# Transformer layer on one core: weight maxima taken across partitions by PE turns and a DRAM round trip instead of POOL, filler matmuls in the front, and a hint on the loop's branch

## The reference

```python
x = x + layernorm(attention(layernorm(x)))
x = x + layernorm(ffn(layernorm(x)))

def attention(x):                       # 16 heads of 32; latent sizes 128
    c_kv, c_q = x @ W_dkv + b_dkv, x @ W_dq + b_dq
    v = c_kv @ W_uv + b_uv
    q = rotary(c_q @ W_qr + b_qr)       # the non-rotary part has width 0
    k = rotary(x @ W_kr + b_kr)
    return softmax(q @ k.T / sqrt(32)) @ v @ W_o + b_o

def ffn(x):                             # 512 -> 2048 -> 512, fwht = Walsh-Hadamard
    x = fwht(x * SU_ug) / 64
    up, gate = x @ W_up.T * (Wscale_ug[:2048] * 64), x @ W_gate.T * (Wscale_ug[2048:] * 64)
    return (fwht(silu(gate) * up * SU_dp) / 64) @ W_down.T * (Wscale_dp * 64)
```

## Time and profile before

| | us |
|---|---|
| median of three runs | 2049.63 |
| the execution that was profiled | 2057.66 |
| its span, first to last instruction | 2055.8 |
| first loop iteration starts on PE | 404.2 |
| last loop iteration ends on PE | 1738.9 |

### The profile page before, as it was taken

One profiled execution on the slowest core, in us unless ns is written; L12 is line 12 of the kernel. 1 busy time (PEld: TensorE's weight loads), 2 busy tenths in 40 slices (PEclk: granted clock), 3 DMA queues, 4 the chain that ended last, 5 costly groups with the idle time before them and its releaser, 6 DMA issues.

```text
span 2055.8 us, 59485 instructions
## 1 busy us (share of the span) xinstructions
PE 1884.7 (92%) x24328; PEld 1368.8 (67%) x24328; DVE 1265.8 (62%) x2131; ACT 1093.5 (53%) x1731; POOL 938.0 (46%) x962
## 2 busy tenths in 40 slices
PE   1377899999998999899989999899989999999997
PEld 0245554677776776677767777667667777677786
DVE  4566766675676666666667667566667667553322
ACT  1555899655544555455546554455546555454221
POOL 1342555554454445454455445444545446333422
PEclk8678999999999999999999999999999999999999
DMA  6472632564456645764466545564566446443643
GB/s 186 128 245 63 154 94 62 110 165 122 119 142 146 155 119 135 161 150 124 120 146 160 118 119 147 134 160 119 145 155 153 120 128 137 137 117 116 184 146 124
DMA packets 352509, 281.01 MB, mean 137 GB/s; under 512 B 284896, under 2 KB 286048, under 8 KB 351200
## 3 DMA queue, kind: packets, MB, share of 16 engines
q1 hardware_dynamic: 342960, 265.37, 50.4%
q10 hardware_dynamic: 9264, 11.61, 1.8%
HBM read 188.84 MB, written 20.97 MB: 102 GB/s over the span
## 4 chain that ended last, share of the span: by engine, by line
PE 64%; issue 14%; POOL 7%; DMA 5%; ACT 4%; DVE 4%; SPq 2%; POOLq 0%; ACTq 0%; DVEq 0%
PE ps L798 25%; PE ps L822 12%; PE ps L740 4%; PE ps L752 4%; PE ps L768 4%; PE ps L728 4%; PE ps L787 3%; DMA qT<-tok 3%; POOL pr L1385 2%; PE ps L773 2%; PE ps L642 1%; POOL room L1413 1%; SPq L570 1%; DVE mx L1257 1%; PE ps L694 1%
## 5 line engine op out<-in xcount | busy, mean ns | idle before, releaser
L972 ACT ACTIVATE pr<-ps,exp_scale 128x1024 f16<-128x1024 f32 x256 | 285.2, 1114 | 367.7 <-PE ps L752 350.2
L1385 POOL TENSOR_TENSOR pr<-p,pr 128x512 f16<-128x512 f32 x256 | 297.5, 1162 | 325.1 <-ACT p L978 324.9
L1257 DVE TENSOR_REDUCE mx<-ps 128x2 f32<-128x1024 f32 x256 | 312.3, 1224 | 207.7 <-PE ps L740 206.5
L798 PEld LDWEIGHTS ps<-x2T,gate_w 128*128 128x128 f16 x6144 | 366.5, 99 | 47.0 <-issue 10.2
L798 PE MATMUL ps<-x2T,gate_w 128*128 128x128 f16 x6144 | 391.7, 221 | 0.7 <-DMA x2T<-nhl 0.7
L798 PEld LDWEIGHTS ps<-x2T,up_w 128*128 128x128 f16 x6144 | 359.0, 98 | 41.4 <-issue 12.9
L798 PE MATMUL ps<-x2T,up_w 128*128 128x128 f16 x6144 | 385.8, 219 | 0.0
L822 PE MATMUL ps<-room 128*128 128x512 f16 x1536 | 375.1, 380 | 5.7 <-POOL room L1413 5.4
L1413 POOL TENSOR_TENSOR room<-room 128x256 f16<-128x256 f32 x256 | 172.8, 675 | 294.5 <-ACT room L1008 293.3
L1003 ACT ACTIVATE room<-ps,half_gate 128x256 f32<-128x256 f32 x256 | 121.8, 476 | 278.6 <-PE ps L798 257.8
L1271 DVE TENSOR_TENSOR pr<-ps,pr 128x512 f16<-128x512 f32 x256 | 175.1, 684 | 130.7 <-ACT ps L983 130.6
(11 more groups left out here) (178 smaller groups left out, 2457.7 us busy)
## 6 DMA issues: line engine op xcount, KB each, us to landing
room<-down_mid SPq DMA_DIRECT2D x256, 512.0 KB, 3.6
xa<-in_x SPq DMA_DIRECT2D x32, 256.0 KB, 3.5
xr<-in_x SPq DMA_DIRECT2D x32, 256.0 KB, 3.8
y_mid<-xr SPq DMA_DIRECT2D x32, 256.0 KB, 2.2
room<-y_mid ACTq DMA_DIRECT2D x32, 256.0 KB, 3.7
out<-room SPq DMA_DIRECT2D x24, 256.0 KB, 2.3
x2T<-in_W_gate SPq DMA_DIRECT2D x5, 1024.0 KB, 6.6
gate_w<-in_W_down SPq DMA_DIRECT2D x4, 1024.0 KB, 4.9
```

The lines of the kernel that those rows point to most:

```text
L798: mm = nc.tensor.matmul(ffn_ps[i % 2][:, col:col + P], weights[:, chunks[j // 4], kt, pw, j % 4 * P:(j % 4 + 1) * P], x2T[:, px, kt, t * P ...
L972: nc.scalar.activation(pr[:, U % 2, 0].rearrange("p (j h) q -> p j (h q)", j=2), work[k], ACT.Exp, scale=exp_scale[:, 0:1]).then_inc(p_hi. ...
L1257: nc.vector.tensor_reduce(mx[:, 2 * tp:2 * tp + 2, h], work[k], AX.X, ALU.max).then_inc(sm_freed.sem, 1)
L1385: nc.gpsimd.tensor_tensor(lo, p32[:], hi, ALU.subtract).then_inc(p_low.sem, 1)
```

## The change

**Maxima over partitions.** The four POOL steps are gone. For the attention weights PE turns the column of maxima into a row (`aturn`, a float32 product with a 128x128 identity), DVE reduces the row to one value per matrix and puts these on a diagonal (`adiag`), and PE spreads them over all partitions with a product with ones (`aback`). For the feed-forward weights the maxima of all partitions go to DRAM (`wput`) and come back to every partition as one row (`wget`), which DVE reduces at the start of `dsc` and `fsc` (`over_rows`).

**Filler matmuls.** `warm.n` issues n matmuls of 128x512 on the identity; nothing reads their result. 57 stand in the front, all before the first `dy`.

**Loads of x.** For sequence 0 tiles 2 and 3 go to buffers of their own, and all four loads of x stand in SP's queue ahead of most weights.

```diff
-            with eng.Fori(1, NB - 1) as b:
+            with nc.Fori(1, NB - 1, engines=(eng.engine,), hint_back_edge=True) as b:
...
+            def wput(b, k):
+                sp.wait_ge(w_max[k], 1)
+                sp.dma_start(max_dram[k], small["f_own"][:, (4, 0)[k]:(7, 4)[k]]).then_inc(w_put[k], 16)
+
+            def wget(b, k):
+                sp.wait_ge(w_put[k], 16)
+                sp.dma_start(max_rows[k], max_dram[k].rearrange("p c -> (p c)").partition_broadcast(P)).then_inc(w_all[k], 16)
...
+            def warm(b, n):
+                for k in range(n):
+                    nc.tensor.matmul(ps[:, 6, :].rearrange("p (k n) -> p k n", k=KT), ident[:],
+                                     ident[:].unsqueeze(1).to_broadcast([P, KT, P]), start=True, stop=True)
+
+            def aturn(b, k):
+                lo, n = ((0, C_O), (C_O, 1))[k]
+                if k == 0:
+                    pe.wait_ge(a_max, 5)
+                    pe.wait_ge(a_bias, 1)
+                else:
+                    pe.wait_ge(o_max, 1)
+                nc.tensor.matmul(ps[0:n, 4 + k, 0:P], m_own[:, lo:lo + n], eye32, start=True, stop=True).then_inc(a_turned, 1)
+
+            def aback(b, k):
+                n = (C_O, 1)[k]
+                pe.wait_ge(a_diag, k + 1)
+                nc.tensor.matmul(ps[:, 4 + k, P:P + n], ones32[0:n, :], m_diag[0:n, 0:n],
+                                 start=True, stop=True).then_inc(a_all, 1)
...
+            def adiag(b, k):
+                n = (C_O, 1)[k]
+                dve.wait_ge(a_turned, k + 1)
+                if k:
+                    dve.wait_ge(a_all, k)
+                link(nc.vector.tensor_reduce(m_col[0:n, :], ps[0:n, 4 + k, 0:P], AX.X, ALU.max))
+                ts(m_diag[0:n, 0:n], eye32[0:n, 0:n], m_col[0:n, :], None, ALU.mult).then_inc(a_diag, 1)
...
+            def over_rows(k):
+                lo, n = ((4, 3), (0, 4))[k]
+                dve.wait_ge(w_all[k], 16)
+                link(nc.vector.tensor_reduce(small["f_all"][:, lo:lo + n], max_rows[k].rearrange("q (p c) -> q c p", c=n), AX.X, ALU.max))
...
-            def aall(b):
-                pool.wait_ge(a_max, 5)
-                pool.wait_ge(a_bias, 1)
-                nc.gpsimd.partition_all_reduce(m_all[:, 0:C_O], m_own[:, 0:C_O], P, RMAX).then_inc(a_all, 1)
-
-            def oall(b):
-                pool.wait_ge(o_max, 1)
-                nc.gpsimd.partition_all_reduce(m_all[:, C_O:C_ALL], m_own[:, C_O:C_ALL], P, RMAX).then_inc(o_all, 1)
...
-            def dall(b):
-                pool.wait_ge(d_max, 1)
...
-            def fall(b):
-                pool.wait_ge(f_max, 1)
...
+        def x_tile(b, t):
+            return xr[:, t % 2, :] if first(b) and t > 1 else xa[:, t % 2, :]
```

More of the change, by code:

```diff
@@ new lines @@
+        xs.0@1 arow c.1 adiag.1 xs.1@1 mx.2 hads c.0 mx.3 dmx proj.0 asd mx.4 dsc mx.5 proj.1 smax.0.0 smax.0.1
+        smax.0.2 smax.0.3 smax.0.4 smax.0.5 brow smax.0.6 xn.0@1 smax.0.7 mtok.0 mx.6 v.0 mx.7 v.1 low.0 dyl.0 mx.8
+        low.1 dyl.1 smax.1.0 mx.9 dyl.2 smax.1.1 low.2 dyl.3 smax.1.2 mx.10 dyl.4 mx.11 low.3 dyl.5 smax.1.3 low.4
+        norm.0 dyl.6 smax.1.4 fmx proj.2 dzl.0 low.5 smax.1.5 smax.1.6 dzl.1 smax.1.7 mtok.1 fsc low.6 dyl.7 low.7
+        dzl.2 xs.2@1 norm.1 dzl.3 low.8 low.9 dzl.4 dyl.8 smax.2.0 low.10 smax.2.1 smax.2.2 smax.2.3 xn.1@1 smax.2.4
@@ new lines @@
+        low.11 smax.2.5 dzl.5 norm.2 low.12 dyl.9 xn.2@1 proj.3 low.13 dyl.10 dzl.6 smax.2.6 dzl.7 dyl.11 smax.2.7
+        mtok.2 dyl.12 xs.3@1 low.14 dzl.8 low.15 dyl.13 xn.3@1 dzl.9 norm.3 dyl.14 low.16 dzl.10 low.17 smax.3.0
+        dyl.15 smax.3.1 smax.3.2 dzl.11 low.18 c.1@1 dzl.12 low.19 dzl.13 smax.3.3 c.0@1 smax.3.4 dzl.14 low.20
+        smax.3.5 norm.4 proj.0@1 low.21 dzl.15 uhl.0 smax.3.6 smax.3.7 mtok.3 uhl.1 low.22 uhl.2 uhl.3 low.23 uhl.4
+        norm.5 uhl.5 low.24 uhl.6 smax.0.0@1 uhl.7 low.25 smax.0.1@1 low.26 smax.0.2@1 uhl.8 smax.0.3@1 uhl.9 uhl.10
@@ L190 @@
     """,
     POOL="""
-        xs.0 xs.1 xn.0 xn.1 xs.2 aall xs.3 xn.2 xn.3 asl.0 asl.1 oall asl.2 asl.3 asl.4 asl.5 asl.6 asl.7 asl.8 asl.9
-        dall proj.0 tok.0.0 tok.0.1 asl.10 asl.11 cut.0 cut.1 cut.2 cut.3 proj.1 tok.1.0 xs.0@1 tok.1.1 low.0 low.1
-        low.2 low.3 low.4 low.5 fall xs.1@1 xn.0@1 proj.2 norm.0 low.6 low.7 tok.2.0 tok.2.1 low.8 low.9 low.10 low.11
-        norm.1 cut.4 low.12 xs.2@1 norm.2 proj.3 low.13 xn.1@1 low.14 cut.5 tok.3.0 xn.2@1 low.15 tok.3.1 low.16
-        xs.3@1 xn.3@1 low.17 low.18 norm.3 cut.6 low.19 cut.7 norm.4 low.20 low.21 proj.0@1 low.22 low.23 cut.8
@@ L534, in xl @@
                 k = t % 2
[L535 to L536 removed]
+                if first(b):
+                    sp.dma_start(x_tile(b, t), x_v[b, t]).then_inc(xb_in[k] if t > 1 else xa_in[k].sem, 16)
+                    return
+                sp.wait_ge(*x_lo.at(b, t - 2))
                 sp.dma_start(xa[:, k, :], x_v[b, t]).then_inc(xa_in[k].sem, 16)
@@ L543, in rl @@
                 sp.wait_ge(*y_n.at(b, t - 2))
+                if first(b) and t < 2:
+                    sp.wait_ge(*x_lo.at(b, t + 2))
                 sp.dma_start(xr[:, k, :], x_v[b, t]).then_inc(xr_in[k].sem, 16)
@@ L591, in fe @@
                 sp.dma_start(out_v[b, t], yt[:, t % 2, :]).then_inc(out_done[t % 2].sem, 16)
-            parts = dict(lda=lda, ldv=ldv, ldx=ldx, raw=raw_, dst=dst, wl=wl, xl=xl, rl=rl, ln1=ln1, ln2=ln2, stk=stk, stq=stq, oe=oe, fe=fe)
-            ahead = next(i for i, (b, s) in enumerate(FRONT["SP"]) if s[0] != "lda" and not (s[0] == "xl" and s[1] < 2))
+            parts = dict(lda=lda, ldv=ldv, wput=wput, wget=wget, ldx=ldx, raw=raw_, dst=dst, wl=wl, xl=xl, rl=rl, ln1=ln1, ln2=ln2, stk=stk, stq=stq, oe=oe, fe=fe)
+            ahead = next(i for i, (b, s) in enumerate(FRONT["SP"]) if s[0] not in ("lda", "xl"))
             for b, s in FRONT["SP"][:ahead]:
@@ L824, in down @@
                 mm.then_inc(down_done.sem, 1)
-            run(pe, "PE", dict(bos=bos, dy=dy, dz=dz, ut=ut, uh=uh, c=c, v=v_, proj=proj, smax=smax, st=st, av=av, o=o,
+            run(pe, "PE", dict(warm=warm, aturn=aturn, aback=aback, bos=bos, dy=dy, dz=dz, ut=ut, uh=uh, c=c, v=v_, proj=proj, smax=smax, st=st, av=av, o=o,
                          gate=gate, up=up, down=down))
@@ L1423, in fe @@
                 nc.gpsimd.tensor_tensor(yt[:, k, :], yt[:, k, :], ft, ALU.add).then_inc(fin_done.sem, 1)
-            run(pool, "POOL", dict(aall=aall, oall=oall, dall=dall, fall=fall, asl=asl, cut=cut_, xs=xs, xn=xn, proj=proj, tok=tok_, low=low, norm=norm, o=o, oe=oe, ys=ys, yn=yn, hid=hid_, fs=fs, fe=fe))
+            run(pool, "POOL", dict(asl=asl, cut=cut_, xs=xs, xn=xn, proj=proj, tok=tok_, low=low, norm=norm, o=o, oe=oe, ys=ys, yn=yn, hid=hid_, fs=fs, fe=fe))
 _PRE = {"x": "L0_attn_x"} | {n: "L0_attn_" + n for n in (
```

183 lines of the change are left out of this document (96 added, 87 removed).

## The result

The changed kernel takes 2006.08 us, the median of four executions (2001.86 to 2015.84); the kernel before took 2049.48 us on the same chip. The ratio is 0.9779, 95% interval 0.9760 to 0.9798. The forecast was 1975 us with a range of 1957 to 2010: the sign and the range held, but of 75 us that were to be gained 43 came. The measured time also lies above 1957 to 1996, which the forecast gave to the case in which both of its parts work; it is inside the range because that was stretched to take in some of the rivals.

What follows compares the result with a forecast made beforehand. PE was taken to bound the loop, a chain of latencies over all engines the front. Loop 37 plus front 38 gave 75 us, off 2049.6: 1974.6, rounded 1975 us, range 1957 to 2010.

Steps and rivals of the forecast that it cites:

- the case in which both of its parts work: Loop and front both gain as forecast: 1975 us (1957 to 1996), chance 0.72.
- The loop's term: Loop's back edges: the hint removes PE's fetch stops and the half clock behind them, gaining 37 us.
- The place of the head: PE's loop: a shift of 130 leaves about 65 matmuls before the second fetch, so a small rest; not in the sum.
- The rule against the hint: Loop: the skill calls code prefetch purely sequential; by that the loop's term would be 0 in place of 37.
- Rivals 2 and 3: Loop: hint does nothing, 2012 us, chance 0.12; hint brings only the head, second stop stays, 1997 us, chance 0.08.
- Rival 5: Loop: hint displaces prefetch, PE stops inside the body too; 2237 us with ten stops per iteration, chance 0.03.
- `aall`: Front, attention-weight maxima: POOL's hole of 13.7 us replaced by steps of 2.5 us; gain 11.2 (10.2 to 12.7).
- `oall`: Front: without this POOL reduction `asl` follows ACT and ends at 62.5, where `proj.0` started at 72.87; gain 10.3 us.
- `dall`: Front: POOL's rotary sum, at 90.59, could start at 80.6 when DVE's product is there; gain 10.0 us.
- The DRAM round trip: Front, feed-forward maxima: result back at 62 to 70 us, `dsc` due at about 62; cost 0 to 8, taken as 2.
- Fillers and clock: Front: fillers keep PE's clock up in the score steps and parts of `c` and `proj.0`; gain 4 us (-3 to +9).
- `fall` and the rest: Later front: PE's 7.6 us wait for POOL and half clock behind it, gain 8; front sum 41.5 cut to 38.

Runs made afterwards that it cites:

- experiment 9: Changed kernel with SP's loop queue reordered: queries' transpose right behind the keys', a W_down load and a store after it; 1993.32 us, ratio 0.9719.
- Experiments 1 and 7: 1: changed kernel without the hint, ratio 0.9841; 7: kernel before, unhinted, with padding putting PE's loop head at a code block's start, ratio 0.9931.
- experiment 2: Kernel before with the back-edge hint added and nothing else; 2042.59 us, ratio 0.9952 to the kernel before.
- Experiment 6: Changed kernel with the low part of the first latent moved earlier in DVE's stream of the front; 2009.54 us, ratio 0.9784.
- experiment 3: Changed kernel without its 57 filler matmuls; 2015.96 us, ratio 0.9817.

## Why the prediction was right or wrong

**The loop's term, mis-sized: -24.7 for -37.** What was removed was read rightly: the branch, the ten stops and the half clock behind them. The step that failed is "what is late next". The text looked for it only in the fetch that follows the head, and excluded the other engines by their busy shares, which leave out SP, whose busy time no such share shows. The next one late was SP's queue: the wait for the queries took 18.7 us of the loop. With it out of the way (experiment 9) the parts come out as they were worked out: PE's standing still falls from 38.3 to 9.9 us, by 28.4 (forecast 33.1 - 6 = 27.1), and its busy time by 11.3 (1295.86 to 1284.59, forecast 10.2 of clock), together 39.7 for 37. The row that told it stood in the trace of before, at 415.82.

**The place of the head.** The forecast took the shift by 130 instructions as luck that makes the rest small, and gave the whole of the 37 to the hint. Experiments 1 and 7 show that the shift alone takes 16 to 18 us in the profiled loops, and experiment 2 that the hint takes the second stop also where the head lies badly. The two overlap: each is worth less where the other is already in.

**The rule against the hint.** The branch of 0.38 us, against 4.76 in the same kernel without the hint, decides: a prefetch by hint works here. (The Trainium skill's "Runtime: NRT & Kernel Launch", "Instruction fetch mechanics", speaks of purely sequential prefetch, which this trace doesn't bear out for a hinted branch.) Rivals 2 and 3 fell with that. Rival 5 fell in the body, where the longest stop without a reason is 0.16 us. The exit's 4.62 us was booked at nothing; that it comes from the hint as rival 5 has it is not shown.

**`aall`, 8.6 for 11.2.** Its replacement took 31.43 to 33.95, the 2.5 us of the forecast. But the maxima were ready 2.8 us later than before (31.43 against 28.62, the start of POOL's hole), and this is the step of the term that failed: "I count nothing". The last load that the maxima need was no later, it landed at 24.60 and before at 26.12. But the rotation table, the last of the eight small loads that the bias step waits for together, landed at 24.60 instead of 15.73, and in DVE's new order four of the five reductions of attention weights stand behind that step, 4.06 us at 27.31. Their weights had landed between 18.19 and 24.16 while DVE stood still for 6.33 us. In the trace of before the bias step starts at the same time, with four of the five done ahead of it and one behind:

```profile
24.66 0.86 DVE L1062 TENSOR_SCALAR pr<-v 128x128 f32<-128x128 f32 x4
...
27.91 0.68 DVE L1033 TENSOR_REDUCE v<-gate_w 128x1 f32<-128x512 f32 x1
```

No experiment put them back ahead of it.

**`oall`, 14.7 at `proj.0` for 21.5.** The eighth `asl` ended at 52.14, so POOL did what was said. PE was not ready: 5.07 us for DVE, 2.5 for a latent at half clock (5.30 against 2.75), 2.8 for fillers. Experiment 6 shows that more than one chain ends there, since taking away the first of these waits brought up the next.

**`dall`, 11.3 for 10.0**, from `proj.0` to the rotary sum: 72.87 to 90.59 before, 58.15 to 64.57 now. **The DRAM round trip, 0 for -2**: the two DMAs took 3.6 and 5.5 us to landing, and DVE's reduction of the row at 70.37 waited for nothing.

**Fillers and clock, -4.5 for +4: the largest error of the front.** Between the first scores and the first `st` 24.48 us became 28.94. The fillers were not the reason (experiment 3 has the first `st` at 105.09 and the same start of the loop). The last two DVE rows of after show one: at 92.47 a step that takes 0.54 us elsewhere lasts 2.92 and ends at 95.39, and at 96.56 one of 0.21 lasts 3.92 and ends at 100.48. POOL's products of 128x2048 beside them end at 95.10 and 100.41. In all ten profiled executions with the new front the first or both of these steps are long, each time beside such a product, and end 0.07 to 0.3 us behind it; the second of them takes 0.21 us in the six in which no such product runs beside it. In the kernel before the same step (0.21 us) starts where POOL's rotary sum ends, at 119.77. (The Trainium skill, "SBUF — State Buffer", "Who interferes with whom", has a lock on a port pair that DVE and GpSimd share, held for a whole instruction, and names `tensor_scalar`; the trace agrees, 3.7 us for one step.) By that the two cost 2.4 + 3.7 = 6.1 us on the way to the first `st`. No experiment moved POOL's product away, so this is read from durations, not shown by an edit.

**`fall` and the rest, 7.7 for 4.5** (8 less the 3.5 that were not to arrive). PE's wait of 7.6 is 4.8 now, and the loop's start gained 29.0 where the first `st` had gained 21.3.

**The signs.** Of the signs that the forecast gave itself, the first score product (76.49 us for 68 to 76), the branch (0.38 us for under 0.3) and half clock (none was to be left behind the back edges and during `smax`) say that it was off. The loop's start of 373.9 is inside 354 to 382, a range wide enough for the front's term to miss by 9 us.
